# Eight batches of selective scan, mixture of experts and gated FFN: the first loads reordered, and the normalisations computed by ScalarE instead of VectorE

## The chip, the cores and the metric

The kernel runs on one core of one Trainium2 chip. The time is device microseconds of one execution. A core has five engines that run side by side, each working through its own list of instructions in order: TensorE (PE in the profile; PEld is its weight load), VectorE (DVE), ScalarE (ACT), GpSimd (POOL) and SyncE (SP, which here only issues DMAs). They meet at semaphores: an instruction adds to one when it is done, and an engine whose next instruction wants a value that is not there yet stands still with everything behind it.

## The reference

x has 8 batches of 1024 tokens of 128 features. Per batch:

```python
delta = softplus(x @ Wd + bd);  Bm = x @ WB + bB;  Cm = x @ WC + bC;  A = -exp(A_log)   # 16 states
h_t = clip(exp(min(delta_t * A, 2)) * h_(t-1) + clip(delta_t * B_t, -2, 2) * x_t, -100, 100)
y_t = sum over the states of h_t * C_t, + x_t * D_param
routing = softmax(y @ Wr + br)                       # 4 experts, the best one is taken
moe = best weight * (silu(y @ up_w + up_b) @ down_w + down_b)
attn = layernorm(y + moe) * ln_w + ln_b
x1  = layernorm(x + attn)
out = layernorm(x1 + (silu(x1 @ wg.T) * (x1 @ wu.T)) @ wdn.T)      # int8 weights times 1/127
```

So each token is normalised three times: (v - mean) * rstd with rstd = (variance + eps) ** -0.5, over its 128 features.

## The kernel before

The work of a batch is cut in four stages: P makes delta, B and C of the batch, A is the scan over its 16 states, B is router, experts and the first two normalisations, C is the FFN and the third. Iteration i runs P of batch i+1, A of batch i, B of batch i-1 and C of batch i-2 side by side. i goes from -1 to 9; 3 to 6 are one hardware loop (four turns), the others are written out. i = 8 and 9 have no scan any more, only B and C.

An iteration has 16 scan steps s, and each is cut in two half steps. The order of all that is not the scan is written out by hand in four tables, PE_STEPS, ACT_STEPS, DVE_STEPS and POOL_STEPS: (half step, stage, task, arguments). The half steps 2s and 2s+1 stand on VectorE behind the scan and behind the product of step s. One scan step is, on VectorE:

- L629: psB = dx * psB, where TensorE has spread row s of B over 128 partitions in PSUM (L370 psB);
- L820: state = scan of decay and psB over the 1024 tokens (decay by ScalarE, L545);
- L829: prod = state * psC (psC again from TensorE, L370), which GpSimd adds up (L899 yacc).

TensorE makes psB of step s+1 when the scan of step s has read the last, and psC of s+1 when the product of s has. Between them, in its own order, stand the matmuls of the experts (L425 up, L439 down), of the FFN (L458, L459 up, L467 down), of delta and B, C (L385 z and bc) and the transposes (L448 x_turn). They use four PSUM banks U0, U1, D and T in turn; a bank is filled again when ScalarE or VectorE has emptied it. ScalarE empties U0 and U1 (L563 silu, L575 gate, L504 z_copy, L511 bc_copy), VectorE D and T (L736 weigh, L751, L777).

A normalisation is task ("norm", c, n): half c of the batch (4 blocks of 128 tokens), n = 0, 1, 2. Before it VectorE takes the statistics ("stats" and "ff_sum": L757, L762, L765) into mv and ve, GpSimd makes rstd = ve ** -0.5 of 128x4 numbers ("rstd", L871), and VectorE then does the four blocks:

```python
if name == "norm":
    c, n = args
    src, dst = ((moe, moe), (attn, x1), (x2, x2))[n]
    dve.wait_ge(rstd_ready[c], 3 * b + n + 1)
    for j in range(NJ):
        ins = v.tensor_scalar(dst[:, c, j, :], src[:, c, j, :], mv[:, c, j, 0:1],
                              rstd[:, c, j:j + 1], ALU.subtract, ALU.mult)
    ins.then_inc(normed[c], 1)
```

Behind n = 0 follows "affine" on GpSimd (times ln_w, plus ln_b, plus x), behind n = 1 the x_turn on TensorE, behind n = 2 the store. A full iteration has six normalisations: (1,0) at half step 4, (0,2) at 9, (1,1) at 11, (0,0) at 19, (1,2) at 24 and (0,1) at 26; (0,0) and (0,1) are of stage B, the others of stage C.

At the start SyncE issues 16 loads of constants on one semaphore, the three FFN weights, three rows of down_b and then the first x (xT). All engines wait for the 16 loads; TensorE and GpSimd also for consts_ready = 2, which VectorE reaches behind its casts of the FFN weights and its four copies of the bias (L618).

Of the kernel before, what the change touches and what calls it, by code (L numbers as in the profile page):

```python
# [943 lines left out]
```

## Time and profile before

| | |
|---|---|
| median of 3 runs | 1146.07 us (1145.62 to 1146.14) |
| the profiled execution | 1146.76 us |
| its span in the trace | 1145.0 us |
| PE busy | 856.6 us, 75% |
| DVE busy | 972.5 us, 85% |
| ACT busy | 536.3 us, 47% |
| POOL busy | 546.0 us, 48% |
| granted clock of TensorE, mean | 0.874 |

The span is from the first to the last instruction in the trace. Busy time says how full an engine is and not whether the end waits for it; for that one reads the chain that ended last, and the order of time with each instruction's idle time in front of it. In rows in order of time the columns are start, length, engine, line, operation, out<-in, how many merged, and in brackets the idle time before and what ended it. In rows by stretch they are the stretch, its length and then busy time with the number of instructions for each engine, the granted clock, the DMA share and GB/s. In groups of instructions: busy time, mean ns of one, then the idle time before them and what ended most of it.

### The profile page before, as it was taken

To read this page: it belongs to the slowest core of one execution; us is meant where nothing else is said; L and a number is where in the kernel's file an instruction comes from. 1 tells how busy PE (TensorE), PEld (TensorE's weight loads), DVE (VectorE), ACT (ScalarE), POOL (GpSimd) and SP (SyncE) were. 2 spreads that over 40 slices of the span, in tenths; PEclk is the share of its full clock that TensorE was granted. 3 is DMA by queue.
4 is the path that set the end of the run, shared out by engine and by line. 5 is a ranking of instruction groups with operands and counts; after the bars stand their busy time and mean duration, and the time that the engine had idled before them with its cause. 6 is when DMAs were issued, how large, how long until landed. Compare 5 with 4: busy or idle time off the path is not lost.

```text
span 1145.0 us, 12832 instructions
## 1 busy us (share of the span) xinstructions
PE 856.6 (75%) x4120; PEld 532.6 (47%) x4120; DVE 972.5 (85%) x1364; ACT 536.3 (47%) x646; POOL 546.0 (48%) x316
## 2 busy tenths in 40 slices
PE   0254499659877788869788688878789688879983
PEld 0110155446445554545446454545446455646662
DVE  2499988899999999998999899998999999884244
ACT  0716067345654257444664256444664254425320
POOL 0145445554555465463664455463665454463222
PEclk9655599879989899888989799988999798899996
DMA  4100010001000100001000100001000000000000
GB/s 125 37 0 1 3 53 1 1 0 47 19 1 10 47 10 10 1 10 46 19 0 10 46 10 9 0 9 47 19 0 10 28 10 11 1 19 19 1 10 19
DMA packets 23038, 20.60 MB, mean 18 GB/s; under 512 B 2227, under 2 KB 19891, under 8 KB 22966
## 3 DMA queue, kind: packets, MB, share of 16 engines
q1 hardware_dynamic: 22966, 19.84, 5.4%
q14 instruction: 52, 0.43, 0.1%
q8 instruction: 20, 0.33, 0.1%
HBM read 15.64 MB, written 4.19 MB: 17 GB/s over the span
## 4 chain that ended last, share of the span: by engine, by line
DVE 52%; PE 24%; issue 18%; ACT 2%; DVEq 1%; DMA 1%; SPq 1%; POOL 1%; POOLq 0%; ACTq 0%
DVE state L820 16%; DVE psB L629 11%; PE psD L439 7%; DVE prod L829 5%; DVE x L771 5%; PE psU L425 4%; DVE bst L757 3%; PE psB L370 2%; PE psU L458 2%; PE psT L439 2%; DVE moe L771 2%; PE psU L385 2%; DVE weighed L736 2%; DVE mv L762 1%; PE psU L459 1%
## 5 line engine op out<-in xcount | busy, mean ns | idle before, releaser
L899 POOL TENSOR_TENSOR yacc<-prod,yacc 128x1024 f32<-128x1024 f32 x112 | 271.5, 2424 | 264.2 <-DVE prod L829 263.8
L820 DVE TENSOR_TENSOR_SCAN state<-decay,psB 128x1024 f32<-128x1024 f32 x128 | 292.7, 2287 | 13.6 <-DVE psB L629 0.5
L563 ACT ACTIVATE hid<-psU,upb_sb 128x512 f32<-128x512 f32 x256 | 175.7, 687 | 264.4 <-PE psU L425 264.3
L425 PE MATMUL psU<-y,up_sb 128*128 128x512 f32 x512 | 254.8, 633 | 1.1 <-ACT hid L563 1.1
L370 PE MATMUL psB<-bc_parts,sel 128*128 128x512 bf16 x256 | 94.2, 456 | 141.4 <-DVE state L820 113.6
L439 PEld LDWEIGHTS psD<-down_sb,hid 128*128 128x128 f32 x1280 | 173.8, 218 | 9.7 <-issue 4.5
L439 PE MATMUL psD<-down_sb,hid 128*128 128x128 f32 x1280 | 172.0, 300 | 0.0
L629 DVE TENSOR_TENSOR psB<-dx,psB 128x1024 f32<-128x1024 f32 x128 | 156.5, 1222 | 10.4 <-PE psB L370 8.5
L829 DVE TENSOR_TENSOR prod<-state,psC 128x1024 f32<-128x1024 f32 x128 | 155.8, 1217 | 9.0 <-PE psC L370 3.2
L425 PEld LDWEIGHTS psU<-y,up_sb 128*128 128x128 f32 x512 | 91.7, 200 | 134.3 <-ACT hid L563 92.7
L545 ACT ACTIVATE decay<-next_delta,a_sb 128x1024 f32<-128x1024 f32 x128 | 136.3, 1135 | 1.5 <-DVE state L820 1.4
L370 PE MATMUL psC<-bc_parts,sel 128*128 128x512 bf16 x256 | 88.4, 432 | 34.5 <-DVE prod L829 34.0
L370 PEld LDWEIGHTS psB<-bc_parts,sel 128*128 128x128 bf16 x256 | 20.3, 103 | 189.0 <-DVE state L820 144.7
L871 POOL TENSOR_TENSOR rstd<-ve,minus_half 128x4 f32<-128x4 f32 x48 | 48.9, 1018 | 111.2 <-DVE ve L765 111.1
L864 POOL TENSOR_TENSOR moe<-moe,weighed 128x512 f32<-128x512 f32 x48 | 72.2, 1503 | 61.3 <-DVE weighed L736 59.6
L439 PEld LDWEIGHTS psT<-down_sb,hid 128*128 128x128 f32 x768 | 89.5, 192 | 4.9 <-issue 2.6
L439 PE MATMUL psT<-down_sb,hid 128*128 128x128 f32 x768 | 89.6, 275 | 0.0
L569 ACT ACTIVATE x1h<-psT 128x512 fp32r<-128x512 f32 x16 | 9.6, 597 | 170.1 <-PE psT L448 170.1
L370 PEld LDWEIGHTS psC<-bc_parts,sel 128*128 128x128 bf16 x256 | 23.5, 104 | 79.6 <-DVE prod L829 54.4
L899 POOL TENSOR_TENSOR yacc<-prod,xD 128x1024 f32<-128x1024 f32 x8 | 18.8, 2354 | 74.6 <-DVE prod L829 74.6
L785 DVE SCALAR_TENSOR_TENSOR hh<-psU,hh 128x512 f32<-128x512 f32 x48 | 32.2, 687 | 24.6 <-PE psU L459 23.5
L736 DVE TENSOR_TENSOR weighed<-psD,top_w 128x512 f32<-128x512 f32 x40 | 27.1, 677 | 25.1 <-PE psD L439 25.0
(115 smaller groups left out, 1101.8 us busy)
## 6 DMA issues: line engine op xcount, KB each, us to landing
xT_sb<-in_xT SPq DMA_DIRECT2D x8, 512.0 KB, 3.5
x_again<-in_xT SPq DMA_DIRECT2D x8, 512.0 KB, 4.3
xt<-in_x SPq DMA_DIRECT2D x16, 256.0 KB, 3.5
out<-x SPq DMA_DIRECT2D x16, 256.0 KB, 2.3
up_sb<-in_up_w SPq DMA_DIRECT2D x1, 1024.0 KB, 7.8
hid<-in_wg SPq DMA_DIRECT2D x1, 192.0 KB, 9.7
hid<-in_wu SPq DMA_DIRECT2D x1, 192.0 KB, 4.4
hid<-in_wdn SPq DMA_DIRECT2D x1, 192.0 KB, 5.1
```

The costliest lines, as they stand in the source:

```text
L370: mm = pe.matmul(half(ps, c), sel[:, which * S + s, :], half(bc_parts, c), start=True, stop=True)
L425: pe.matmul(bank[banks[f]][:, :], up_sb[:, e, f * 128:(f + 1) * 128], half(y, c), start=True, stop=True).then_inc(filled[banks[f]], 1)
L439: mm = pe.matmul(bank[d][:, j * 128:(j + 1) * 128], hid[:, k % 2, f, j * 128:(j + 1) * 128], down_sb[:, e * NF + f, :], start=False, stop= ...
L545: nc.scalar.activation(decay[:, s % NDECAY, :], next_delta[:, :], ACT.Exp, scale=a_sb[:, s:s + 1]).then_inc(decay_ready, 1)
L563: nc.scalar.activation(hid[:, k % 2, f, :], bank[u][:, :], ACT.Silu, bias=upb_sb[:, (k % E) * NF + f:(k % E) * NF + f + 1]).then_inc(drain ...
L629: v.tensor_tensor(psB[:, :], dx[:, :], psB[:, :], ALU.mult).then_inc(inp_ready, 1)
L736: v.tensor_tensor(weighed[:, k % 2, :, :], by_token(d), top_w[:, c * NJ:(c + 1) * NJ, e:e + 1].to_broadcast([128, NJ, D]), ALU.mult).then_ ...
L771: ins = v.tensor_scalar(dst[:, c, j, :], src[:, c, j, :], mv[:, c, j, 0:1], rstd[:, c, j:j + 1], ALU.subtract, ALU.mult)
L820: v.tensor_tensor_scan(state[:, :], decay[:, s % NDECAY, :], psB[:, :], 0.0, ALU.mult, ALU.add).then_inc(state_ready, 1)
L829: v.tensor_tensor(prod[:, s % NPROD, :], state[:, :], psC[:, :], ALU.mult).then_inc(prod_ready, 1)
L864: g.tensor_tensor(dst, ytok[:, c * NJ:(c + 1) * NJ, 0:D] if e == 0 else dst, weighed[:, k % 2, :, :], ALU.add).then_inc(mixed, 1)
L899: g.tensor_tensor((y if s == S - 1 else yacc)[:, :], prod[:, s % NPROD, :], (xD if s == 0 else yacc)[:, :], ALU.add).then_inc(added, 1)
```

## The change

Three edits, in one kernel.

1. The first x and the eight constants that stages P and A need are issued first, the eight on a semaphore of their own (first_in); the FFN weights and down_b follow, and the eight other constants come last. TensorE starts when first_in and the cast identb are there; VectorE makes a_max before it waits for the FFN weights; TensorE and GpSimd wait for the rest of VectorE's setup before the first scan iteration, and all four for the late constants before the first iteration with stage B. The bias rows are staged in y and weighed instead of rest and inp.
2. The task "norm" leaves DVE_STEPS and stands in ACT_STEPS at the same half steps, as four activations Identity(rstd * v + shift) with two pointer operands.
3. GpSimd's task "rstd" makes shift = -mean * rstd in two more multiplications of 128x4.

```diff
@@ ACT_STEPS @@
-    (4, 'B', 'router_exp'), (4, 'A', 'decay', 4, 9), (8, 'B', 'silu', 2), (9, 'B', 'silu', 3),
-    (10, 'P', 'z_copy'), (11, 'A', 'decay', 9, 12), (12, 'P', 'bc_copy'), (12, 'P', 'softplus'),
+    (4, 'B', 'router_exp'), (4, 'C', 'norm', 1, 0), (4, 'A', 'decay', 4, 9), (8, 'B', 'silu', 2), (9, 'B', 'silu', 3),
+    (9, 'C', 'norm', 0, 2), (10, 'P', 'z_copy'), (11, 'C', 'norm', 1, 1), (11, 'A', 'decay', 9, 12), (12, 'P', 'bc_copy'), (12, 'P', 'softplus'),
...
@@ sync @@
+            sp_.dma_start(xT_sb[:, :], xT[0]).then_inc(xT_in, 16)
+
             for dst, src in (
-                (wd_sb[:, :], wd), (wbc_sb[:, :], wbc), (bd_sb[:, :], bd), (bbc_sb[:, :], bbc),
...
+                (wd_sb[:, :], wd), (wbc_sb[:, :], wbc), (ident, ident_c), (bd_sb[:, :], bd), (bbc_sb[:, :], bbc),
+                (a_sb[:, :], a_log), (dpar[:, :], d_param), (selcol[:, :], sel_c),
             ):
-                sp_.dma_start(dst, src).then_inc(consts_in, 16)
+                sp_.dma_start(dst, src).then_inc(first_in, 16)
...
             for row in (0, 64, 96):
-                sp_.dma_start(rest[row:row + 1, 0:E * D], down_b).then_inc(bias_rows_in, 16)
+                sp_.dma_start(y[row:row + 1, 0:E * D], down_b).then_inc(bias_rows_in, 16)
+
+            for dst, src in (
+                (ident_wr[:, D:DE], wr), (rev_sb[:, :], rev_c.to_broadcast([128, E])),
...
+                (down_sb[:, :, :], down_w.rearrange("e (n p) d -> p (e n) d", p=128)),
+            ):
+                sp_.dma_start(dst, src).then_inc(consts_in, 16)
@@ tensor @@
+                if first_scan(it):
+                    pe.wait_ge(setup_dve, SETUP)
+                if first_moe(it):
+                    pe.wait_ge(consts_in, 16 * LATE)
...
-            pe.wait_ge(consts_in, 16 * 16)
-            pe.wait_ge(consts_ready, 2)
+            pe.wait_ge(first_in, 16 * FIRST)
+            pe.wait_ge(setup_dve, SETUP_IDENTITY)
@@ scalar @@
+                if name == "norm":
+                    c, n = args
+                    src, dst = ((moe, moe), (attn, x1), (x2, x2))[n]
+                    act.wait_ge(rstd_ready[c], 3 * b + n + 1)
+                    for j in range(NJ):
+                        ins = nc.scalar.activation(dst[:, c, j, :], src[:, c, j, :], ACT.Identity,
+                                                   bias=shift[:, c, j:j + 1], scale=rstd[:, c, j:j + 1])
+                    ins.then_inc(normed[c], 1)
@@ gpsimd @@
-                    g.tensor_tensor(rstd[:, c, :], ve[:, c, :], minus_half[:, :], ALU.pow).then_inc(rstd_ready[c], 1)
+                    g.tensor_tensor(minus_mean[:, c, :], mv[:, c, :, 0], minus_one[:, :], ALU.mult
+                                    ).then_inc(rstd_steps, 1)
+                    g.tensor_tensor(rstd[:, c, :], ve[:, c, :], minus_half[:, :], ALU.pow).then_inc(rstd_steps, 1)
+                    pool.wait_ge(rstd_steps, 2)
+                    pool.sem_clear(rstd_steps)
+                    g.tensor_tensor(shift[:, c, :], minus_mean[:, c, :], rstd[:, c, :], ALU.mult
+                                    ).then_inc(rstd_ready[c], 1)
```

ScalarE's list at half steps 9 to 12 of a loop turn, where two normalisations come in a short stretch (hid is the silu of the experts, zb the z_copy, decay the operand of the scan, bcf the bc_copy). Before:

```order
L563 ACTIVATE hid<-psU,upb_sb 128x512 x2
L503 REGISTER_ALU
L504 ACTIVATE zb<-psU,bd_sb 128x512 x2
L286 REGISTER_ALU
L545 ACT_TABLE_LOAD
L545 ACTIVATE decay<-next_delta,a_sb 128x1024
```

and now:

```order
L587 ACTIVATE hid<-psU,upb_sb 128x512 x2
L597 REGISTER_ALU
L599 ACTIVATE x<-x,shift,rstd 128x128 x4
L526 REGISTER_ALU
L527 ACTIVATE zb<-psU,bd_sb 128x512 x2
L597 REGISTER_ALU
L599 ACTIVATE x<-attn,shift,rstd 128x128 x4
L291 REGISTER_ALU
L569 ACT_TABLE_LOAD
L569 ACTIVATE decay<-next_delta,a_sb 128x1024
```

One normalisation stands ahead of the copy that empties U0 and U1, one behind it and ahead of decay and bc_copy; no table load is added.

GpSimd's list at half steps 7 to 12 (moe the mixing of the experts, yacc the sum of the products, rest an operand of stage P). Before:

```order
L864 TENSOR_TENSOR moe<-moe,weighed 128x512
L899 TENSOR_TENSOR yacc<-prod,yacc 128x1024
L871 TENSOR_TENSOR rstd<-ve,minus_half 128x4
L899 TENSOR_TENSOR yacc<-prod,yacc 128x1024
L846 TENSOR_TENSOR rest<-bcf,parts 128x1024
```

and now:

```order
L898 TENSOR_TENSOR moe<-moe,weighed 128x512
L945 TENSOR_TENSOR yacc<-prod,yacc 128x1024
L905 TENSOR_TENSOR minus_mean<-mv,minus_one 128x4
L907 TENSOR_TENSOR rstd<-ve,minus_half 128x4
L909 ISA
L910 TENSOR_TENSOR shift<-minus_mean,rstd 128x4
L945 TENSOR_TENSOR yacc<-prod,yacc 128x1024
L880 TENSOR_TENSOR rest<-bcf,parts 128x1024
```

Each rstd has become three operations with a wait inside, at the same place among the sums.

## Rows read from the trace of the kernel before

**Rows 1.** The chain that ended last, shares of the span by engine (the page).

```profile
DVE 52%; PE 24%; issue 18%; ACT 2%; DVEq 1%; DMA 1%; SPq 1%; POOL 1%; POOLq 0%; ACTq 0%
```

**Rows 2.** One loop turn by engine: stretch, length, PE, PEld, DVE, ACT, POOL busy.

```profile
517.00:646.80 129.80, 105.22 (x515) 67.08 (x515) 121.27 (x168) 67.61 (x81) 68.82 (x39) 0.91 0.05 17
```

**Rows 3.** Line L771 in three stretches: stretch, length, DVE busy (instructions).

```profile
140.00:254.00 114.00, 5.25 (x8) 0.87 0.04 15
...
517.00:646.80 129.80, 14.03 (x24) 0.91 0.05 17
...
907.00:1026.00 119.00, 13.72 (x24) 0.89 0.04 11
```

**Rows 4.** The start (instructions in order of time: start, length, engine, instruction, idle).

```profile
4.51 0.43 SPq L316 DMA_DIRECT2D selcol<-in_sel  x1
...
18.66 0.22 ACT L493 ACTIVATE a_sb<-a_sb 128x16 f32<-128x16 f32 x1 [16.63 <-DMA down_sb<-in_down_w]
...
19.00 2.29 DVE L603 CAST sel<-selcol 128x4096 bf16<-128x4096 f32 x1
...
24.87 1.28 DVE L618 COPY bias_down<-inp 128x512 bf16<-128x512 bf16 x4
...
26.59 3.75 PE L385 MATMUL psU<-xT_sb,wd_sb 128*128 128x512 f32 x4 [26.59 <-DVE peak L621]
```

**Rows 5.** DMA issues: KB each, median us from issue to landing.

```profile
selcol<-in_sel SPq DMA_DIRECT2D x1, 16.0 KB, 1.7
...
hid<-in_wdn SPq DMA_DIRECT2D x1, 192.0 KB, 5.1
```

**Rows 6.** VectorE in one loop turn (instructions in order of time).

```profile
558.19 3.14 DVE L771 TENSOR_SCALAR x<-x,mv,rstd 128x128 f32<-128x128 f32 x4
...
572.87 1.22 DVE L829 TENSOR_TENSOR prod<-state,psC 128x1024 f32<-128x1024 f32 x1
...
598.86 1.23 DVE L629 TENSOR_TENSOR psB<-dx,psB 128x1024 f32<-128x1024 f32 x1
...
622.19 1.22 DVE L629 TENSOR_TENSOR psB<-dx,psB 128x1024 f32<-128x1024 f32 x1
...
626.34 2.07 DVE L771 TENSOR_SCALAR x<-attn,mv,rstd 128x128 f32<-128x128 f32 x4
```

**Rows 7.** TensorE in the same turn.

```profile
564.92 0.61 PE L370 MATMUL psB<-bc_parts,sel 128*128 128x512 bf16 x2 [2.44 <-DVE state L820]
...
570.86 0.59 PE L370 MATMUL psC<-bc_parts,sel 128*128 128x512 bf16 x2
...
597.07 0.50 PE L458 MATMUL psU<-x1h,wu_sb 128*128 128x512 f32 x1 [2.69 <-DVE hh L785]
...
620.65 0.59 PE L370 MATMUL psB<-bc_parts,sel 128*128 128x512 bf16 x2
```

**Rows 8.** ScalarE in the same turn.

```profile
560.36 0.69 ACT L563 ACTIVATE hid<-psU,upb_sb 128x512 f32<-128x512 f32 x1 [0.17 <-PE psU L425]
...
581.14 0.60 ACT L569 ACTIVATE x1h<-psT 128x512 fp32r<-128x512 f32 x1 [5.60 <-PE psT L448]
```

**Rows 9.** ScalarE's forms (line, shapes, count, busy, mean ns, idle before).

```profile
L563 ACT ACTIVATE hid<-psU,upb_sb 128x512 f32<-128x512 f32 x256 | 175.7, 687 | 264.4 <-PE psU L425 264.3
...
L575 ACT ACTIVATE hh<-psU 128x512 f32<-128x512 f32 x48 | 28.4, 597 | 40.8 <-PE psU L459 40.6
...
L552 ACT ACTIVATE ytok<-psT 128x396 f32<-128x396 f32 x8 | 4.0, 500 | 42.6 <-PE psT L418 42.6
```

**Rows 10.** GpSimd's groups of instructions by line.

```profile
L871 POOL TENSOR_TENSOR rstd<-ve,minus_half 128x4 f32<-128x4 f32 x48 | 48.9, 1018 | 111.2 <-DVE ve L765 111.1
...
L879 POOL TENSOR_TENSOR moe<-moe,lnw_sb 128x512 f32<-128x512 f32 x16 | 20.5, 1278 | 8.4 <-DVE moe L771 8.4
...
L846 POOL TENSOR_TENSOR rest<-bcf,parts 128x1024 f32<-128x1024 f32 x8 | 17.1, 2136 | 51.2 <-ACT parts L516 51.2
```

**Rows 11.** TensorE in the last 25 us.

```profile
1125.42 1.12 PE L448 MATMUL psT<-ident_wr,x 128*128 128x128 f32 x4 [8.72 <-DVE x L771]
```

More of the change, by code:

```diff
@@ L46 @@
 FIRST_FULL, LAST_FULL = 3, 6
+FIRST, LATE = 8, 8
+SETUP_IDENTITY, SETUP = 7, 20
 Y_GROUPS = [(0, 3), (3, 6), (6, 8)]
@@ L232, in ssm_moe_ffn_kernel @@
         rstd = sb("rstd", [128, 2, NJ])
+        minus_mean = sb("minus_mean", [128, 2, NJ])
+        shift = sb("shift", [128, 2, NJ])
+        minus_one = sb("minus_one", [128, NJ])
         psB = pb("psB", [D, L])
@@ L238, in ssm_moe_ffn_kernel @@
         drained = {n: sem(f"drained_{n}") for n in bank}
+        first_in = sem("first_in")
         consts_in = sem("consts_in")
@@ L286, in wait, with first_scan, first_moe @@
                 eng.wait_ge(s, value)
+        def first_scan(it):
+            return isinstance(it.b["A"], int) and it.b["A"] == 0
+        def first_moe(it):
+            return isinstance(it.b["B"], int) and it.b["B"] == 0
         def iterate(eng, body):
@@ L490, in _ @@
         def _(act):
-            act.wait_ge(consts_in, 16 * 16)
+            act.wait_ge(first_in, 16 * FIRST)
             nc.scalar.activation(a_sb[:, :], a_sb[:, :], ACT.Exp).then_inc(setup_act, 1)
@@ L594, in setup @@
                 dve.wait_ge(setup_dve, steps[0])
-            setup(v.memset(rest[:, 0:E * D], 0.0))
+            setup(v.memset(y[:, 0:E * D], 0.0))
             setup(v.memset(ones_col[:, :], 1.0))
             setup(v.memset(minus_half[:, :], -0.5))
+            setup(v.memset(minus_one[:, :], -1.0))
             setup(v.memset(limits[:, 0:2], SAFE_B))
             setup(v.memset(limits[:, 2:3], SAFE_H))
-            dve.wait_ge(consts_in, 16 * 16)
+            dve.wait_ge(first_in, 16 * FIRST)
             setup(v.tensor_copy(identb[:, :], ident))
             setup(v.tensor_copy(sel[:, :, :], selcol[:, :].rearrange("p (s o) -> p s o", o=1).to_broadcast([128, 2 * S, 128])))
+            assert steps[0] == SETUP_IDENTITY + 1
+            dve.wait_ge(consts_ready, 1)
+            setup(v.tensor_reduce(a_max[:, :], a_sb[:, :], X, ALU.max))
+            v.memset(peak[:, :], 0.0).then_inc(consts_ready, 1)
+            dve.wait_ge(consts_ready, 2)
             dve.wait_ge(ff_in, 48)
@@ L610, in _ @@
             dve.wait_ge(bias_rows_in, 48)
-            row = rest[:, 0:E * D]
-            part = inp[:, 0:E * D // 2].bitcast(BF16)
+            row = y[:, 0:E * D]
+            part = weighed[:, 0, :, :].rearrange("p j d -> p (j d)")[:, 0:E * D // 2].bitcast(BF16)
             setup(v.tensor_copy(part, row))
@@ L618, in _ @@
                 setup(v.tensor_copy(bias_down[:, :, j, :], part.rearrange("p (e d) -> p e d", e=E)))
-            dve.wait_ge(consts_ready, 1)
-            setup(v.tensor_reduce(a_max[:, :], a_sb[:, :], X, ALU.max))
-            v.memset(peak[:, :], 0.0).then_inc(consts_ready, 1)
-            dve.wait_ge(consts_ready, 2)
+            assert steps[0] == SETUP
             def wide(t, n, d):
@@ L755, in run @@
                         src = x2
+                    wait(dve, rstd_ready[c], 3 * b + n)
                     for j in range(NJ):
@@ L765, in run @@
                     v.tensor_scalar(ve[:, c, :], mv[:, c, :, 1], EPS, None, ALU.add).then_inc(stats_steps[c], 1)
-                if name == "norm":
-                    c, n = args
-                    src, dst = ((moe, moe), (attn, x1), (x2, x2))[n]
-                    dve.wait_ge(rstd_ready[c], 3 * b + n + 1)
-                    for j in range(NJ):
-                        ins = v.tensor_scalar(dst[:, c, j, :], src[:, c, j, :], mv[:, c, j, 0:1],
-                                              rstd[:, c, j:j + 1], ALU.subtract, ALU.mult)
-                    ins.then_inc(normed[c], 1)
                 if name == "x_low":
@@ L887, in body @@
                 b = it.b["A"]
+                if first_scan(it):
+                    pool.wait_ge(setup_dve, SETUP)
+                if first_moe(it):
+                    pool.wait_ge(consts_in, 16 * LATE)
                 for s in range(S):
```

21 lines of the change are left out of this document (11 added, 10 removed), and 18 rows, old and new, of tables (ACT_STEPS, DVE_STEPS).

## The prediction

> **What bounds the kernel now.** I read the chain that ended last first: over half of the span lies on VectorE, a quarter on TensorE, and ScalarE and GpSimd have 3% together [rows 1]. Then one turn of the loop by engine: of 129.8 us VectorE is busy 121.3, TensorE 105.2, ScalarE 67.6, GpSimd 68.8 [rows 2]. So VectorE sets the pace in the scan iterations, but TensorE is only 25 us behind it, and a part of those is made up of waits for VectorE's scans and products. The reader should see that at most 16 us a turn can be won on VectorE before TensorE binds, and less if the two alternate. After the last scan (from about 1026 us) TensorE carries nearly everything, and behind its last FFN the chain runs from engine to engine.
>
> **The start.** SyncE issues one load each 0.47 us; the ninth goes out at 4.51 [rows 4]. The changed kernel puts x and eight constants in these nine places. A small one lands 1.7 us after its issue [rows 5], so first_in is complete near 6.3, the cast identb (0.2 us) near 6.6, and I take 6.9 for the first matmul of z. It started at 26.59 [rows 4]: 19.7 us are won. ScalarE, which had waited 16.63 us for down_sb, is free as early [rows 4]. What is late next is VectorE's setup: it starts at 6.4 instead of 18.7, but the last FFN weight, issued near 5.9, lands 5.1 us later [rows 5], at 11.0; the three casts (1.2 us, three gaps included) and the eight bias operations up to the end of L618 (24.87 + 1.28 = 26.15 [rows 4], from 22.51: 3.6 us) bring it to about 16. Its first task, the maximum of B, stood 7.5 us behind z's start and is wanted at 14.4; it comes 1.6 late, but nothing on the path waits for it until 8 us later. The sel cast of 2.29 us [rows 4] lies in the wait for the weights. The bulk loads of 2 MB come behind all this and are needed 100 us later. The first scan iteration has no normalisation and moves as a block. Bounds: 17 us, if the 512 KB of x hold the small loads back by what the slowest of those nine could take, to 20. I take 19.6.
>
> **The normalisations off VectorE.** They cost it 5.25 us in iteration 1 (8 instructions), 14.03 in a full turn (24), 13.72 in iteration 7 [rows 3]. How much of that the end sees is read slot by slot in the turn from 517 to 646.8.
>
> - (1,0), 1.1 us at 537.4: VectorE's next external need was there before; all 1.1 is won.
> - (0,2) and (1,1), 3.14 us at 558.19 and 3.16 at 566.09 [rows 6]: here TensorE takes over. VectorE alone would bring the product of step 6 from 572.87 [rows 6] to 565.5. But its psC came at 570.86 + 0.59 = 571.45 [rows 7], so 1.4 us were slack, and the row ahead of it in TensorE's list is shortened only by the 1.1 from above and by its wait of 2.44 us for the scan of step 5 [rows 7]. Against it stands ScalarE: the normalisation is now between the last silu (to 561.05 [rows 8]) and the copy that empties U0 and U1 for TensorE, and moves that copy by about 1.6 less the 0.6 it stood idle and the rest of TensorE's slack: 0.5. So 1.1 + 2.4 + 1.4 - 0.5 = 4.4 us, (1,0) included, of 7.4.
> - (0,0), 3.15 us at 593.26: its next instructions, the FFN products, need TensorE's matmuls of up; the last of these had waited 2.69 us for VectorE [rows 7]. Both move, less 0.3: 2.8 won, read at the multiplication that started at 598.86 [rows 6].
> - (1,2), 1.43 us at 619.72: psB was ready at 620.65 + 0.59 = 621.24 [rows 7] for a multiplication at 622.19 [rows 6]: 0.9 won.
> - (0,1), 2.07 us at 626.34 [rows 6]: VectorE bound, 2.07 won.
>
> Sum 10.2; I take 10.0 a turn. Five turns (i = 2 and the four of the loop) give 50. Iteration 7 has no z and bc, whose matmuls and copies stand in the second slot: 13 of its 13.7. Iteration 1 has only (0,0) and (0,1), and TensorE had waits at both: 5.2.
>
> **What is added.** On ScalarE 192 activations. No row has 128x128; from 128x396 in 500 ns to 128x512 in 597 is 0.84 ns a column [rows 9], so 128 columns take 276 with constant operands; a pointer bias made 597 into 687 [rows 9], and here are two pointers: 456. Four take 1.1 us (no pointer charge) to 1.8 (nothing overlaps); I take 1.6, nearest to the rows with pointers. 48 of them are 77 us on an engine that has more than 600 idle, and the price is only what stands behind them: the 0.5 above, and the long row of decay, bc_copy and softplus behind (1,1). It has 5.60 us of idle time at its end, ahead of x_high [rows 8]; 3.2 us of work and the 4.4 us that everything else moves earlier use this up, and the 1.28 us of table load behind it had its own gap: 0 to 1 us a turn, taken as the 0.2 rounded off above.
>
> The Trainium skill, "ScalarE: Activation LUTs", What ACT_TABLE_LOAD costs, gives 186 ns plus 0.833 per column and about 93 for each pointer operand, with 93 of overlap; that is an estimate of 1.64 us for four, and with it the sum stays. The traces' 90 ns between 597 and 687 agree.
>
> On GpSimd 96 multiplications of 128x4. Not in the trace either: the power of the same shape takes 1018 ns, 512 columns of ordinary arithmetic 1278 and 1024 columns 2136 [rows 10], which extrapolates to 0.42 at zero columns. Bounds 0.1 to 1.0 each, I take 0.4, so 0.8 to 0.9 for each rstd with its wait. In the scan iterations this lies in GpSimd's idle half: rstd (1,1) ended at 561.7, and ScalarE reaches it 1.5 us after that.
>
> **The drain.** After the scans nothing is won on VectorE. In i = 8 TensorE is bound and its waits do not come from the normalisations. In i = 9 three stand in line on the path ((1,0), (1,1), (1,2)); TensorE waited 8.72 us for the second [rows 11]. Each becomes longer by 0.9 on GpSimd and 1.6 - 1.12 = 0.5 on ScalarE: 3 x 1.4 = 4 us lost.
>
> **Sum**, against the profiled execution of 1146.76 us (its span of 1145.0 and 1.8 around it; 0.7 over the median of the runs): 1146.8 - 19.6 - 5.2 - 50 - 13 + 4 = 1063.
>
> **Rivals.**
>
> A. TensorE's and ScalarE's order gives less: each normalisation on ScalarE delays a copy that TensorE waits for, and a turn gains 6 instead of 10, iteration 7 nine. For it: TensorE is already at 81% of a turn [rows 2]. Against: only one of six stands ahead of such a copy. 1063 + 20 + 4 = 1087.
>
> B. TensorE follows VectorE freely, and the whole VectorE time goes: 5 x 14.03 + 13.7 + 5.2. For it: waits of TensorE that shrink may keep its clock up, since it was granted 0.91 in the turn [rows 2] and its matmuls are slowest behind its waits. Against: rows 7. 1063 - 20 - 1 = 1042.
>
> C. The wait for GpSimd comes back. Four blocks took 1.1 us where GpSimd was idle and 3.14 beside its sums [rows 6], so of the 14.03 us about 5.9 were waits. If the next VectorE instructions meet the sums instead, a turn gains 4. Against: behind each stands a multiplication with a PSUM operand, 1.22 us everywhere. 1063 + 5 x 5.9 = 1092. The Trainium skill, "GPSIMD Engine Reference", Specifications, has GpSimd's SBUF interfaces shared with VectorE for instructions in a two-port mode or with two SBUF inputs; by that rule the multiplications by psB and psC are spared and the sum stays, and the trace, with 1.22 in every slot, agrees.
>
> D. The early start does not come, because the loads of x and the FFN weights share the queue and first_in waits for all of x behind the weights: 1063 + 15 = 1078.
>
> E. Slower than before: ScalarE stands at a normalisation whose shift is not there, and behind it in its list the copies of z and of B, C wait, and with them TensorE. The place is (0,2) or (1,1), half steps 9 and 11. It decides the sign only from 84 / 6 = 14 us lost in each of the six iterations that have both slots; with 17 us, 1063 + 6 x 17 = 1165. Against: (0,2)'s rstd was ready 10 us before ScalarE comes to it; the three operations would have to take that long.
>
> **How the numbers follow.** Forecast 0.68, A 0.13, B 0.11, C 0.04, D 0.03, E 0.01. The range stops 3 us short of B and 1 short of A, which leaves out less than 2 in 10: 1045 to 1086. No change to be told means within 0.2%, about 2.3 us. Faster: all but E and a small rest, 0.97; same 0.01; slower 0.02.
>
> **What would show it.** The first matmul at about 7 us and the first scan at 34.6 instead of 54.3. A loop turn of 119.8 us, VectorE busy 107 of it, ScalarE 77. Four activations in 1.6 us; minus_mean and shift at 0.4 each. A wait of VectorE for psC in step 6 that was not there, and TensorE without its 2.4 us wait before psB of step 6. The end of the last scan iteration 88 us earlier than before, and the drain 4 us longer. I am wrong if a turn is above 122 or under 117, or if ScalarE is seen waiting for shift in the loop.

## The result, and the profile after

The changed kernel takes **1071.97 us** (median of 4 runs, 1068.56 to 1072.54), the kernel before 1145.84 beside it on the same chip: a ratio of 0.9351, 95% interval 0.933 to 0.9372. The forecast was 1063 with 1045 to 1086; 9 of the 84 us that it promised did not come.

The page of the changed kernel, engines and chain of waits; the chain answers to [rows 1]:

```profile
PE 839.0 (78%) x4059; PEld 523.2 (49%) x4120; DVE 877.5 (82%) x1173; ACT 610.2 (57%) x838; POOL 561.4 (52%) x412
...
PE 37%; DVE 36%; issue 15%; ACT 8%; POOL 2%; DVEq 1%; SPq 0%; DMA 0%; ACTq 0%; POOLq 0%
```

VectorE's share of the chain fell from 52% to 36% and TensorE's rose from 24 to 37: neither alone bounds the kernel now, the two alternate. One turn of the loop (i = 5; the turn of [rows 2] is i = 4), in the same columns:

```profile
596.75:719.31 122.56, 103.51 (x507) 66.42 (x515) 108.31 (x144) 76.70 (x105) 70.71 (x51) 0.90 0.06 18
```

VectorE is busy 108.3 us of it (107 were forecast), ScalarE 76.7 (77), but the turn is 122.6 long and not 119.8. VectorE lost 13.0 us of work and 5.7 of that came back as idle time. The prediction gave a turn above 122 as a sign that it is wrong. Two of the five turns are above it (122.8 for i = 3, 122.6 for i = 5), the others take 120.2 to 121.7: the sign is there.

For a ledger I take the start of VectorE's first copy of an iteration (bc_parts, L793 before and L827 after) as the border between iterations, and the start of the last product as the end of the scans. All from the profiled executions:

| stretch | before | after | won | forecast |
|---|---|---|---|---|
| to the first border | 51.15 | 31.32 | 19.8 | 19.6 |
| i = 0 | 86.96 | 87.38 | -0.4 | 0 |
| i = 1 | 115.96 | 113.29 | 2.7 | 5.2 |
| i = 2 to 6 | 650.26 | 607.56 | 42.7 | 50 |
| i = 7, to the last product | 122.18 | 106.92 | 15.3 | 13 |
| drain, to the span's end | 118.49 | 123.13 | -4.6 | -4 |
| span | 1145.0 | 1069.6 | 75.4 | 83.8 |

The start, instructions in order of time; they answer to [rows 4]:

```profile
4.52 0.44 SPq L324 DMA_DIRECT2D selcol<-in_sel  x1
...
6.34 0.22 ACT L516 ACTIVATE a_sb<-a_sb 128x16 f32<-128x16 f32 x1 [4.30 <-DMA selcol<-in_sel]
...
6.68 2.29 DVE L639 CAST sel<-selcol 128x4096 bf16<-128x4096 f32 x1
...
6.74 3.75 PE L402 MATMUL psU<-xT_sb,wd_sb 128*128 128x512 f32 x4 [6.74 <-DVE identb L638]
...
12.89 1.28 DVE L659 COPY bias_down<-weighed 128x512 bf16<-128x512 bf16 x4
```

The first matmul stands at 6.74 instead of 26.59 (6.9 forecast), and VectorE's setup ends at 12.89 + 1.28 = 14.2 (16 forecast): the last FFN weight, 5.1 us in [rows 5], lands in 2.9.

The new operations, groups by line (count, busy, mean ns, idle before):

```profile
L907 POOL TENSOR_TENSOR rstd<-ve,minus_half 128x4 f32<-128x4 f32 x48 | 48.9, 1020 | 0.0
L599 ACT ACTIVATE x<-attn,shift,rstd 128x128 f32<-128x128 f32 x64 | 26.3, 488 | 0.1
L599 ACT ACTIVATE x<-x,shift,rstd 128x128 f32<-128x128 f32 x64 | 26.3, 485 | 15.0 <-POOL shift L910 15.0
...
L905 POOL TENSOR_TENSOR minus_mean<-mv,minus_one 128x4 f32<-128x4 f32 x48 | 9.7, 202 | 107.3 <-DVE ve L804 107.3
L910 POOL TENSOR_TENSOR shift<-minus_mean,rstd 128x4 f32<-128x4 f32 x48 | 9.6, 201 | 8.2 <-POOL rstd L907 8.2
```

ScalarE's idle time before L599 is waiting for a shift: 15.0 us in two places of the drain, and 7.1 in the moe group (not shown), of which this one is in iteration 1 and the rest, 6.3, in the drain. In the loop it never waited for one, as forecast.

```profile
182.73 1.65 ACT L599 ACTIVATE moe<-moe,shift,rstd 128x128 f32<-128x128 f32 x4 [0.81 <-POOL shift L910]
```

Now the turn, in the places of [rows 6 to 8]. TensorE and VectorE around step 6:

```profile
641.16 0.59 PE L387 MATMUL psB<-bc_parts,sel 128*128 128x512 bf16 x2
642.07 1.98 PE L402 MATMUL psU<-xT_sb,wbc_sb 128*128 128x512 f32 x4 [0.31 <-ACT zb L527]
...
647.90 0.38 PE L387 MATMUL psC<-bc_parts,sel 128*128 128x512 bf16 x1
```

```profile
648.31 1.22 DVE L863 TENSOR_TENSOR prod<-state,psC 128x1024 f32<-128x1024 f32 x1 [2.90 <-PE psC L387]
```

TensorE's wait of 2.44 us before psB is gone, and VectorE waits 2.90 us for psC, which it had not done before: TensorE has taken over here. The product stands at 648.31 - 596.75 = 51.6 us into the turn, before at 572.87 - 517.02 = 55.9: 4.3 won, 4.4 forecast. Four steps later ScalarE, and then VectorE (with its row of iteration 1 ahead):

```profile
668.93 1.64 ACT L599 ACTIVATE moe<-moe,shift,rstd 128x128 f32<-128x128 f32 x4
670.59 1.28 ACT L569 ACT_TABLE_LOAD   x1
671.88 4.27 ACT L569 ACTIVATE decay<-next_delta,a_sb 128x1024 f32<-128x1024 f32 x4
```

```profile
190.07 1.31 DVE L710 SCALAR_TENSOR_TENSOR next_delta<-zb,sp 128x1024 f32<-128x1024 f32 x1 [2.62 <-ACT decay L569]
...
671.25 1.22 DVE L667 TENSOR_TENSOR psB<-dx,psB 128x1024 f32<-128x1024 f32 x1
672.58 2.29 DVE L854 TENSOR_TENSOR_SCAN state<-decay,psB 128x1024 f32<-128x1024 f32 x1
...
676.19 1.23 DVE L710 SCALAR_TENSOR_TENSOR next_delta<-zb,sp 128x1024 f32<-128x1024 f32 x1 [1.32 <-ACT decay L569]
```

The multiplication at 671.25 is 74.5 us into the turn (81.8 before): 7.3 won, with 4.4 + 2.8 = 7.2 forecast. Then VectorE stands at L710, which overwrites next_delta and must wait until ScalarE's decay of states 12 to 15 has read it; that decay now stands behind normalisation (0,0). In the kernel before the same two instructions were

```profile
594.90 4.27 ACT L545 ACTIVATE decay<-next_delta,a_sb 128x1024 f32<-128x1024 f32 x4
...
602.40 1.20 DVE L672 SCALAR_TENSOR_TENSOR next_delta<-zb,sp 128x1024 f32<-128x1024 f32 x1
```

The decay ended at 599.17, 3.2 us before VectorE came to the delta. VectorE now comes to it 7.3 us earlier in the turn, but ScalarE, with the normalisation in front, ends the decay only 2.8 us earlier: the 3.2 us of slack are used up and 1.3 us are waited. Behind that wait, TensorE (start, length, idle before; below it stretches with PE, PEld, DVE, ACT, POOL busy and then the granted clock):

```profile
686.01 0.38 PE L387 MATMUL psB<-bc_parts,sel 128*128 128x512 bf16 x1 [3.48 <-DVE state L854]
686.23 5.29 PE L442 MATMUL psU<-y,up_sb 128*128 128x512 f32 x8
...
692.01 3.84 PE L442 MATMUL psU<-y,up_sb 128*128 128x512 f32 x8
```

```profile
679.80:686.00 6.20, 2.73 (x25) 2.65 (x25) 5.93 (x10) 0.00 (x0) 1.78 (x1) 1.00 0.00 0
686.20:691.50 5.30, 5.30 (x10) 2.02 (x10) 4.60 (x13) 2.06 (x3) 2.88 (x5) 0.68 0.01 2
```

```profile
696.32 1.23 DVE L667 TENSOR_TENSOR psB<-dx,psB 128x1024 f32<-128x1024 f32 x1 [1.50 <-PE psB L387]
```

TensorE has waited 3.48 us for the scan that the waiting delta held up; behind the wait its granted clock is 0.68, the mean of a stretch partly at the lower of its two levels (1.2 GHz of 2.4), the matmuls of ("up", 6), expert 2 for the second half of the batch, take 5.29 us where those of ("up", 7) take 3.84, and VectorE waits 1.50 us more for the psB behind them. The wait at L710 is paid more than once.

### The profile page after: what moved, and what is told of

It reads as the page before. It is cut to its first block, busy times and chain, and to the rows that moved or that the text cites. A ratio compares the mean times of both kernels' runs of the same rounds, so it can differ in the third digit from the quotient of the medians.

```text
span 1069.6 us, 12973 instructions
## 1 busy us (share of the span) xinstructions
PE 839.0 (78%) x4059; PEld 523.2 (49%) x4120; DVE 877.5 (82%) x1173; ACT 610.2 (57%) x838; POOL 561.4 (52%) x412
## 4 chain that ended last, share of the span: by engine, by line
PE 37%; DVE 36%; issue 15%; ACT 8%; POOL 2%; DVEq 1%; SPq 0%; DMA 0%; ACTq 0%; POOLq 0%
PE psU L442 15%; DVE state L854 12%; DVE psB L667 8%; PE psD L456 6%; DVE prod L863 3%; PE psU L475 3%; PE psB L387 3%; ACT decay L569 2%; DVE bst L796 2%; DVE weighed L774 2%; PE psU L402 2%; PE psU L476 2%; PE psT L456 2%; PE psC L387 1%; DVE top_w L761 1%
## 5 line engine op out<-in xcount | busy, mean ns | idle before, releaser
L854 DVE TENSOR_TENSOR_SCAN state<-decay,psB 128x1024 f32<-128x1024 f32 x128 | 292.8, 2287 | 13.2
L442 PE MATMUL psU<-y,up_sb 128*128 128x512 f32 x512 | 265.5, 656 | 0.6 <-ACT hid L587 0.6
L387 PE MATMUL psB<-bc_parts,sel 128*128 128x512 bf16 x233 | 83.7, 438 | 130.7 <-DVE state L854 102.2
L863 DVE TENSOR_TENSOR prod<-state,psC 128x1024 f32<-128x1024 f32 x128 | 156.0, 1219 | 22.3 <-PE psC L387 15.8
L667 DVE TENSOR_TENSOR psB<-dx,psB 128x1024 f32<-128x1024 f32 x128 | 156.6, 1224 | 16.5 <-PE psB L387 15.0
L456 PEld LDWEIGHTS psD<-down_sb,hid 128*128 128x128 f32 x1280 | 161.9, 205 | 7.3 <-issue 2.7
L442 PEld LDWEIGHTS psU<-y,up_sb 128*128 128x128 f32 x512 | 95.8, 206 | 139.5 <-ACT hid L587 92.8
L456 PE MATMUL psD<-down_sb,hid 128*128 128x128 f32 x1280 | 161.3, 288 | 0.2
L387 PE MATMUL psC<-bc_parts,sel 128*128 128x512 bf16 x222 | 78.4, 425 | 20.3 <-DVE prod L863 18.5
L905 POOL TENSOR_TENSOR minus_mean<-mv,minus_one 128x4 f32<-128x4 f32 x48 | 9.7, 202 | 107.3 <-DVE ve L804 107.3
L607 ACT ACTIVATE hh<-psU 128x512 f32<-128x512 f32 x48 | 28.5, 598 | 41.6 <-PE psU L476 41.2
L593 ACT ACTIVATE x1h<-psT 128x512 fp32r<-128x512 f32 x16 | 9.6, 597 | 73.9 <-PE psT L465 73.7
```

The source lines that it names most:

```text
L387: mm = pe.matmul(half(ps, c), sel[:, which * S + s, :], half(bc_parts, c), start=True, stop=True)
L442: pe.matmul(bank[banks[f]][:, :], up_sb[:, e, f * 128:(f + 1) * 128], half(y, c), start=True, stop=True).then_inc(filled[banks[f]], 1)
L456: mm = pe.matmul(bank[d][:, j * 128:(j + 1) * 128], hid[:, k % 2, f, j * 128:(j + 1) * 128], down_sb[:, e * NF + f, :], start=False, stop= ...
L667: v.tensor_tensor(psB[:, :], dx[:, :], psB[:, :], ALU.mult).then_inc(inp_ready, 1)
L854: v.tensor_tensor_scan(state[:, :], decay[:, s % NDECAY, :], psB[:, :], 0.0, ALU.mult, ALU.add).then_inc(state_ready, 1)
L863: v.tensor_tensor(prod[:, s % NPROD, :], state[:, :], psC[:, :], ALU.mult).then_inc(prod_ready, 1)
```

## Experiments

All were timed in interleaved rounds with the kernel before. "Ratio" is against that kernel; medians of the kernel before were 1146.26, 1145.75 and 1145.33 us in the three sets.

**1. The start alone** (the changed kernel's loads and setup; the four tables and the normalisation as before).

> The changed start alone; the normalisations stay on VectorE and GpSimd makes rstd only. Theory (the two edits add up, and the start is a pure shift): the first scan begins at 34.4 us as in the changed kernel, everything behind it stands as before, 19.8 us less: 1126 us. Rival (the start only looks like a gain because the normalisations left VectorE idle enough to use it): gain under 15 us, above 1131.

Measured 1127.61 us (1126.64 to 1128.41), ratio 0.9841 [0.9824, 0.9858]: 18.7 won. The term of 19.6 stands, and D is refuted.

**2. The normalisations alone** (loads and setup as before).

> The normalisations on ScalarE alone, with the start as it was. Theory (the edits add up): 75.4 of span less 19.8 = 55 to 56 us gained, 1090 us, loop turns of 120 to 123 us as in the changed kernel, and the wait of VectorE's delta for ScalarE's decay is there six times. Rival (late constants and transfers of the new start disturb iteration 1, where 2.7 us came instead of 5.2): iteration 1 gains 5 us here, and the time is 1087 or less.

Measured 1090.04 (1088.0 to 1091.82), ratio 0.9505 [0.9487, 0.9523]: 56.2 won. 18.7 + 56.2 = 74.9, the whole change gave 73.9: the two parts add up within the spread of the runs. Iteration 1 took 113.4 us here too, so its shortfall does not come from the start.

**3. The delta later in VectorE's list.**

```diff
-    ..., (19, 'C', 'ff_mul', 1), (20, 'P', 'delta'), (20, 'B', 'weigh', 4), (21, 'B', 'stats', 0, 1),
-    (21, 'B', 'weigh', 5), (22, 'C', 'ff_sum', 1), ...
+    ..., (19, 'C', 'ff_mul', 1), (20, 'B', 'weigh', 4), (21, 'B', 'stats', 0, 1),
+    (21, 'B', 'weigh', 5), (21, 'P', 'delta'), (22, 'C', 'ff_sum', 1), ...
```

> The changed kernel with one entry of VectorE's list moved: delta stands behind weigh 5 in half step 21 instead of ahead of weigh 4 in half step 20. Theory (delta waits for the last decay of the running batch, which now stands behind a normalisation on ScalarE, and that wait is what was missing: 8.7 us in six waits, and TensorE, which then waits 3.5 us for the next scan, runs at the lower clock behind it): the wait is gone, psB of step 12 is waited for 2 us or less, a loop turn falls from 122.5 to 120 or below, 1072 - 6 x 1.45 - up to 5 x 1.5 = 1056 to 1063. Rival (TensorE is the bound there and delta's wait only covers its own): within 3 us of the changed kernel, 1069 or more.

Measured **1058.12** (1057.13 to 1059.3), ratio 0.9231 [0.9217, 0.9245]: 13.9 us under the changed kernel. Its turn from 592.04 to 711.43, TensorE where psB of step 12 is, and the clock there:

```profile
592.04:711.43 119.39, 101.10 (x507) 65.12 (x515) 108.27 (x144) 76.61 (x105) 70.59 (x51) 0.93 0.06 18
...
679.95:683.70 3.75, 3.75 (x10) 1.36 (x9) 3.16 (x12) 2.06 (x3) 1.37 (x3) 1.00 0.01 2
```

```profile
679.73 0.38 PE L387 MATMUL psB<-bc_parts,sel 128*128 128x512 bf16 x1 [2.19 <-DVE state L854]
679.95 3.78 PE L442 MATMUL psU<-y,up_sb 128*128 128x512 f32 x8
```

VectorE in step 6 of the same turn:

```profile
643.34 1.22 DVE L863 TENSOR_TENSOR prod<-state,psC 128x1024 f32<-128x1024 f32 x1 [2.81 <-PE psC L387]
```

VectorE does the same 108.3 us of work, the wait for decay is gone from all iterations, TensorE's wait is 2.19 instead of 3.48, its clock stays at 1.00 and the up takes 3.78. The wait for psC of step 6 is still there. The five turns i = 2 to 6 last 597.4 us together, 119.5 each: against before 52.9 are won, 10.6 a turn. Against the changed kernel they are 10.2 us shorter, where 6.1 us of the wait for decay stood.

**4. Normalisation (0,0) back on VectorE** (out of ScalarE's list, into VectorE's at half step 19; delta where it was).

> The changed kernel with one of the six normalisations of an iteration, (0,0), back on VectorE at its old place; GpSimd still makes shift. Theory (delta's wait comes from this normalisation on ScalarE): the wait of delta is gone, but 3.1 us of VectorE come back in each of 7 iterations, and 1.45 in 6 of them are given back, with them the slower clock behind: 1072 + 7 x 3.1 - 6 x 1.45 - 5 x 1.5 = 1078, between 1074 and 1086. Rival (the wait comes from elsewhere in ScalarE's list): the wait stays and the time is 1072 + 22 = 1094.

Measured 1081.9 (1079.63 to 1083.32), ratio 0.9437 [0.9419, 0.9454]: 10 us over the changed kernel. The wait for decay is gone here as well, so it came from this normalisation on ScalarE. It does not pay: VectorE has 7 times 3.1 = 21.7 us of work back, of which the time shows 9.9; most of the 14 us that experiment 3 gives are in the difference. Moving the delta gives the same without that price.

**5. Normalisation (0,0) of one block** (on the changed kernel).

```diff
-                    for j in range(NJ):
+                    for j in range(1 if (c, n) == (0, 0) else NJ):
```

> The changed kernel (delta where it was), with normalisation (0,0) of one block of four on ScalarE; three blocks stay unnormalised. ScalarE reaches decay 12 to 15 some 1.15 us earlier, so VectorE's delta, which waited 1.32 us for them, waits about 0.2. Theory: that wait, its doubling on TensorE (3.5 us of idle time before psB of step 12, 1.5 us for the slower up of expert 6) and nothing else made the shortfall: turns of 120 instead of 122.5 and 1059, from 1057 to 1063. If each us of the wait is worth just one us, 1072 - 7 x 1.15 = 1064. Rival (the place of delta in VectorE's list, not the wait, made the 14 us that the late delta gave): 1069 or more.

Measured 1057.69 (1056.62 to 1058.95), ratio 0.9224 [0.9212, 0.9237], 14.3 us under the changed kernel with delta in its old place. What all deltas waited for in the changed kernel (us in total, times, longest), and then, of this kernel, a normalisation and the same sum (us, times):

```profile
DVE next_delta L710 <- ACT decay L569: 8.7, 6, 2.6
```

```profile
663.24 0.48 ACT L599 ACTIVATE moe<-moe,shift,rstd 128x128 f32<-128x128 f32 x1
```

```profile
  ACT decay L569: 2.0, 4
```

So these waits of VectorE fell by 6.7 us, and 14.3 were won by the medians. In the profiles it is 10.5 up to the last product (946.47 to 935.98) and 2.0 in the drain, which have another cause (below). The five turns give 10.1 of it (607.6 to 597.5) for 5.5 us of wait: there each us was worth nearly two. TensorE behind it is as in experiment 3: it waits 2.14 us, and the up takes 3.78. The rival of one for one (1064) is refuted, and so is the one of delta's place in the list (1069 or more). The shorter normalisation also moves ScalarE's later work 1.15 us forward; that this alone is worth nothing was not tried.

**6. GpSimd's two multiplications left out** (on the kernel of 3).

```diff
-                    g.tensor_tensor(minus_mean[:, c, :], mv[:, c, :, 0], minus_one[:, :], ALU.mult
-                                    ).then_inc(rstd_steps, 1)
...
-                    g.tensor_tensor(shift[:, c, :], minus_mean[:, c, :], rstd[:, c, :], ALU.mult
-                                    ).then_inc(rstd_ready[c], 1)
...
-                                                   bias=shift[:, c, j:j + 1], scale=rstd[:, c, j:j + 1])
+                                                   bias=minus_one[:, j:j + 1], scale=rstd[:, c, j:j + 1])
```

> The kernel with the late delta, GpSimd making rstd only; ScalarE's bias is the constant -1, so the mean's shift is left out. It prices the two multiplications of 128x4 (0.20 us each in the trace, and 0.17 between). Theory: off the path in the scan iterations, on it three times in the drain: 1058.1 - 3 x 0.5 = 1056.6, at least 1055 and at most 1058.1, with turns of 119.4 as before. Rival (what GpSimd has to do more comes back to VectorE or ScalarE in the loop as waits, as the prediction's C had it): 1052 or less, with turns under 118.5.

Measured 1055.6 (1055.23 to 1057.28), ratio 0.9213 [0.92, 0.9225]. That is 2.5 us under experiment 3, more than the 1.5 expected, but the intervals of the ratios overlap. The profiles part the two: the drain takes 119.7 us against 121.2, the 1.5 expected, and the five turns 596.8 against 597.4, so nothing of GpSimd's added work is seen in the loop.

**7. Each normalisation as one activation of 128x512** (on the kernel of 3).

```diff
-                    for j in range(NJ):
-                        ins = nc.scalar.activation(dst[:, c, j, :], src[:, c, j, :], ACT.Identity,
-                                                   bias=shift[:, c, j:j + 1], scale=rstd[:, c, j:j + 1])
+                    ins = nc.scalar.activation(dst[:, c, :, :].rearrange("p j d -> p (j d)"),
+                                               src[:, c, :, :].rearrange("p j d -> p (j d)"), ACT.Identity,
+                                               bias=shift[:, c, 0:1], scale=rstd[:, c, 0:1])
```

> The kernel with the late delta, each normalisation as one activation of 128x512 with the first block's two pointers instead of four of 128x128: three blocks get wrong factors. ScalarE spends about 0.78 us on one instead of 1.64. Theory: in the loop ScalarE's time matters only ahead of the copy of z (0.3 us of wait before bc, at most 0.8), in the drain three times: 1058.1 - 2.6 - 2 = 1053.5, from 1051.5 to 1055.5. Rival (ScalarE's time costs nothing in the loop): 1055.5. Rival (ScalarE's added 9.8 us a turn bind the loop in several places): 1048 or less, turns under 118.

Measured 1053.69 (1052.0 to 1055.09), ratio 0.9192 [0.918, 0.9205]. The total is as expected. The five turns take 593.0 us against 597.4, so ScalarE's time costs something in the loop, under 1 us a turn; it does not bind it. The drain as a whole is only 0.3 shorter (121.2 to 120.9), but this profile has 2.0 us of TensorE's low clock in it that the profile of 3 has not (below); from the first ff_down of i = 9 to x_turn, behind that, it takes 12.08 us instead of 13.72. So the shorter normalisations do shorten the drain, by 0.8 us each.

**8. TensorE's up of experts 2 and 3 earlier** (on the kernel of 3).

```diff
-    ... (6, 'B', 'down', 1), (7, 'B', 'up', 2), (9, 'B', 'up', 3), ...
+    ... (6, 'B', 'down', 1), (6, 'B', 'up', 2), (8, 'B', 'up', 3), ...
```

> The kernel with the late delta; TensorE's up of experts 2 and 3 moved ahead of psB of steps 4 and 5 (half steps 6 and 8 instead of 7 and 9), into the 2.94 us in which TensorE waits for the scan before it goes on at 4.86 us for what takes 3.79 elsewhere. Theory (TensorE binds in the first half of a turn, from the scan of step 4 to psC of step 6, where VectorE waits 2.81 us): psC of step 6 comes 0.7 to 2 us earlier in each of six iterations: 1058.1 - 6 x 0.9 = 1053, from 1048 to 1056. Rival (VectorE binds anyway, and psB of step 4, now behind an up, comes late): 1058 or more.

Measured 1061.0 (1060.76 to 1062.65), ratio 0.9259 [0.9246, 0.9271]: 2.9 us slower, a miss. Its TensorE in the turn from 591.54:

```profile
623.62 1.98 PE L442 MATMUL psU<-y,up_sb 128*128 128x512 f32 x4 [0.90 <-ACT hid L587]
...
632.49 0.61 PE L387 MATMUL psC<-bc_parts,sel 128*128 128x512 bf16 x2 [1.97 <-DVE prod L863]
632.93 3.45 PE L402 MATMUL psU<-xT_sb,wd_sb 128*128 128x512 f32 x4
```

The wait before psB of step 4 was filled, but TensorE then stands 1.97 us for the product of step 4, and z behind it takes 3.45 us instead of the 1.88 of experiment 3. The product of step 6 stands 51.4 us into the turn, where experiment 3 has it at 51.3, and the loop's turns are as long. The idle time moved, and the slow matmuls are now behind its new place. The loss is in iterations 1 and 7, 1.6 and 3.2 us longer than in experiment 3, against 1.6 won in iteration 2; why there was not followed.

**9. The copy of z ahead of normalisation (0,2) on ScalarE** (on the kernel of 3).

```diff
-    (9, 'C', 'norm', 0, 2), (10, 'P', 'z_copy'), (11, 'C', 'norm', 1, 1), ...
+    (10, 'P', 'z_copy'), (10, 'C', 'norm', 0, 2), (11, 'C', 'norm', 1, 1), ...
```

> The kernel with the late delta; on ScalarE normalisation (0,2) stands behind the copy of z instead of ahead of it. In the trace with the late delta TensorE waits 0.3 to 0.8 us for that copy before bc, in the stretch that ends in VectorE's wait of 2.81 us for psC of step 6. Theory (the normalisation ahead of the copy costs TensorE this much, and the end sees all of it, as the prediction had it with 0.5): 1058.1 - 6 x 0.6 = 1054.5, from 1053 to 1056.5. Rival (the wait is made up behind, or comes back at (1,1), decay and bc_copy, which now stand later by as much): 1057.5 or more.

Measured 1058.09 (1057.24 to 1059.65), ratio 0.9242 [0.9229, 0.9255]: nothing. The rival holds. The product of step 6, and what stands later in ScalarE's and VectorE's lists:

```profile
640.52 1.22 DVE L863 TENSOR_TENSOR prod<-state,psC 128x1024 f32<-128x1024 f32 x1 [2.29 <-PE psC L387]
...
651.91 0.87 DVE L796 BATCH_NORM_STATS2 bst<-moe 128x6 f32<-128x128 f32 x4 [0.42 <-POOL moe L898]
```

```profile
652.93 1.98 PE L442 MATMUL psU<-y,up_sb 128*128 128x512 f32 x4 [0.59 <-ACT hid L587]
```

VectorE's wait fell from 2.81 us (in experiment 3) to 2.29, and the product stands at 50.8 us into the turn instead of 51.3, so the copy was on the path; but two steps later there are waits of 0.42 and 0.59 us that experiment 3 does not have, and the five turns last 597.4 us in both. The equal totals alone would not show it, since the drain of this profile has the 2.0 us of low clock too (123.1 us long); experiment 11 adds the same edit to a kernel whose drain has none, and gains nothing either.

**10. The drain's normalisations on VectorE** (on the kernel of 3; where no scan runs, VectorE normalises as before and GpSimd makes rstd alone; the edits of ScalarE's, VectorE's and GpSimd's lists in turn).

```diff
-                if name == "norm":
+                if name == "norm" and it.runs["A"]:
...
+                if name == "norm" and not it.runs["A"]:
...
+                    if not it.runs["A"]:
+                        g.tensor_tensor(rstd[:, c, :], ve[:, c, :], minus_half[:, :], ALU.pow
+                                        ).then_inc(rstd_ready[c], 1)
+                        return
```

> The kernel with the late delta; in the two iterations behind the last scan the normalisations are VectorE's again, by tensor_scalar with the mean and rstd as before, and GpSimd makes rstd alone there. Theory (the path there runs through three of them, 2.25 us each from rstd's start to the normalised block before and 3.30 in the changed kernel): 1058.1 - 3 x 1.05 = 1055, from 1053.5 to 1056.5. Rival (the slower drain comes from work that the earlier last scan leaves behind it, not from the form of the normalisation): 1057.5 or more.

Measured **1054.05** (1053.88 to 1054.92), ratio 0.9205 [0.9193, 0.9218], the lowest median of the kernels that leave nothing out: 4.1 us under experiment 3 (3.0 by the ratios) and 17.9 under the changed kernel. From the last product (933.32) to the end of its span (1051.9) it takes 118.6 us; before 118.5, experiment 3 121.2. So the edit is worth 2.6 us. The last product itself stands 3.0 us earlier than in the profile of experiment 3 (936.31), though the two kernels run the same instructions up to there: profiles of equal code differ by that much.

**11. Experiments 9 and 10 together.**

> The late delta, the copy of z ahead of normalisation (0,2), and the drain's normalisations on VectorE. They touch different stretches, so their gains should add: 1058.1 - 3.6 - 3.1 = 1051.4, from 1049.5 to 1054. Rival (one of them takes away what the other gives): 1055 or more.

Measured 1055.43 (1054.22 to 1057.25), ratio 0.9219 [0.9206, 0.9232]: no gain over 10, and the intervals of the two overlap. The sum forecast for it failed with experiment 9's term.

## Why the prediction was right, and where it was not

**The start** (19.6): 19.8 in the trace, 18.7 by itself on the clock. Right, step by step. The FFN weights came sooner than I took them, which nothing used.

**The slots of a turn.** (0,2) with (1,1) and (1,0): 4.3 for 4.4, with the change of bound at step 6 as told (rival A's mechanism in the one place where it was given room). (0,0): 3.0 for 2.8, read at the multiplication where the prediction reads it. What failed is the step behind it: "the price is only what stands behind them: the 0.5 above, and the long row of decay, bc_copy and softplus behind (1,1)". Behind (0,0) in ScalarE's list stands decay 12 to 15, and VectorE's own delta waits for that. The place is not in the list of slots; before, it showed no wait. It took 1.32 us of VectorE in this turn and 2.62 in iteration 1; in the five turns, through TensorE's longer wait and its slower up, it took nearly twice as much (6.1 us of wait, 10.2 us of time in experiment 3). Experiment 3 removed the wait by order and experiment 5 by length, and both came to 1058. Without it a turn gains 10.6, with 10.0 forecast: the slots were sized right, and 1063 would have been 5 us too high for a kernel without this wait. So the sum came within 9 us, far inside a wide range, while its largest term, 50 for the five turns, was 7.3 too high for a reason that the prediction does not have; the 2.3 us more of iteration 7 made up for a part of it by luck. One reading in its first paragraph is loose: the 25 us of TensorE are its distance from the length of the turn; from VectorE's busy time it is 16, the number that the prediction goes on with.

**Iteration 1** (5.2): 2.7, and 4.1 with the late delta in the profile of experiment 3 (111.9 us). In the profiles of experiments 9, 10 and 11, whose lists are the same as experiment 3's in this iteration, it takes 110.6 to 110.8 us, and the whole 5.2 is there. So taking away the wait of delta (2.62 us, lengthened by ScalarE's wait of 0.81 for the shift ahead of the same decay) gives back 1.4 us in one profile and all 2.5 in three; the 1.2 us between them are a difference between profiles of the same code.

**Iteration 7** (13): 15.3. It has no delta of a next batch, so it never had the wait. VectorE's busy time fell by 13.2 us there (113.28 to 100.13) and its idle time by 2.1; why the idle time fell too was not tried.

**What was added.** Four activations take 1.64 us (1.6 taken), so the term held. The Trainium skill, "ScalarE: Activation LUTs", What ACT_TABLE_LOAD costs, gave an estimate of 1.64 us for four, and the trace agrees (1.63 to 1.66; in experiment 5 one alone takes 0.48). The two multiplications take 0.20 us each where 0.4 was taken: extrapolating the line from 512 and 1024 columns to zero gave twice the price. The 0.5 us for the copy of z was real as a wait, and worth nothing in the end (experiment 9).

**The drain** (4): 4.6. The size came out by luck: the normalisations account for 2.7 of it, and TensorE's clock for the rest. Set against the last product, ff_down of i = 9, x_turn behind it, the last ff_down and the end of the span stand at

| | before | after | experiment 3 | experiment 10 |
|---|---|---|---|---|
| first ff_down of i = 9 | 87.25 | 89.28 | 87.24 | 87.27 |
| x_turn | 98.91 | 103.02 | 100.96 | 98.93 |
| last ff_down | 108.12 | 111.80 | 109.82 | 108.25 |
| end | 118.5 | 123.1 | 121.2 | 118.6 |

The three normalisations do stand in line, as forecast. (1,0) and (1,1) lie between the first ff_down and x_turn, which are 11.66 us apart before and 13.74 after: 1.0 each. (1,2) lies behind the last ff_down, and what is left to the end is 10.4 before and 11.4 in experiment 3: 1.0 again. That makes 3.1 and not 3 x 1.4. The part that was sized too high is GpSimd's, 0.9 a piece: without its two multiplications (experiment 6) the first distance is 12.69, so they cost 0.5 each time. ScalarE's 0.5 was right (1.65 against 1.12 for the four blocks). Of the 3.1 us, 0.4 comes back between x_turn and the last ff_down (9.21 us before, 8.78 after), where more of the FFN's matmuls ran at the upper level of the clock.

The other 2.0 us of the changed kernel, before the first ff_down, are TensorE's clock. Two stretches of eight FFN matmuls there, in the changed kernel, and the same matmuls before:

```profile
949.50:953.20 3.70, 3.48 (x8) 2.15 (x8) 0.90 (x2) 1.29 (x3) 0.74 (x1) 0.54 0.00 0
1031.50:1034.90 3.40, 3.40 (x8) 1.50 (x6) 1.38 (x2) 0.66 (x2) 0.00 (x0) 0.52 0.00 0
```

```profile
1029.60:1032.40 2.80, 2.41 (x8) 1.38 (x9) 1.03 (x2) 1.23 (x3) 0.68 (x1) 1.00 0.00 0
1110.40:1112.90 2.50, 2.30 (x8) 0.89 (x6) 1.23 (x2) 0.72 (x2) 0.00 (x0) 1.00 0.00 0
```

Granted 0.54 and 0.52 against 1.00, about 1 us each. The profiles of experiments 7 and 9 have both slow stretches too (the first ff_down stands at 89.25 and 89.22), that of experiment 1 has the first alone (88.35), and all others have neither. The second stretch in experiment 9:

```profile
1017.40:1020.80 3.40, 3.34 (x8) 1.52 (x6) 1.38 (x2) 0.60 (x1) 0.00 (x0) 0.50 0.00 0
```

The drain's code is the same in the changed kernel, in experiment 3 and in experiment 9; what sets the clock there is open.

**Rivals.** A (1087) is refuted as a whole: 42.7 us were won in five turns, not 30. B (1042) too: even without the wait for decay VectorE waits 2.8 us for psC of step 6. C: a turn was to gain only 4 us, and the five gained 8.5 each. VectorE's busy time fell by 13.0 of the 14.03 us of [rows 3], so about 1 us of waits beside GpSimd came back. By the rule of the Trainium skill, "GPSIMD Engine Reference", Specifications, multiplications with a PSUM operand are spared by GpSimd, and the trace agrees: L667 and L863 take 1.20 to 1.23 us in every slot after the change as well. E: ScalarE waited for one shift in all scan iterations, 0.81 us. D fell with experiment 1.

## What to carry to other kernels

When work moves to another engine, list for each place what stands behind it in the new list, and for each of those who waits for it, also where the trace of before shows no wait: a dependence with slack has no row, and this one had 3.2 us of it in a turn in which the waiting engine came 7 us earlier. The loser can be the very engine that was relieved, and if a third engine waits behind it, the wait can be paid again. And a trade that pays where an engine is the bound (the loop) costs where only latency counts (the drain): the two can have different forms, which was worth another 2.6 us here.

## What the runs showed of the hardware that I had not expected

- TensorE's clock after its own waits. Eight matmuls of 128x512 took 5.29 us at a granted 0.68 behind a wait of 3.48 us and 3.78 at 1.00 behind one of 2.19; z took 3.45 behind a wait of 1.97 (experiment 8) and 1.88 without one. In these rows a wait cost its length and up to 1.6 us again. Its length alone does not decide it: before, the four matmuls behind the wait of 2.44 us of [rows 7] (bc) took 1.88.
- The same matmuls of the drain ran at a granted 0.50 to 0.54 in three profiles and at 1.00 in others with the same code there. Two kernels whose totals are compared can differ by 2 us through this alone.
- A GpSimd operation of 128x4 costs 0.20 us as a multiplication and 1.02 as a power, with 0.17 between dependent ones: the operation matters more than the shape.
